# An AdaLN state-space block and six attention and feed-forward layers: output product in three rounded passes, Gelu from PSUM, new orders of the engines' queues, two state rows on GpSimd

## The reference

```python
def _L0_cond_ref(x, t_emb, ...):                # x (128, 32, 128), t_emb (128, 256)
    xr, gate = jnp.split(x @ W_in.T, 2, axis=-1)
    xr = xr + t_emb[:, None, :]
    xc = silu(causal_conv4(xr) + b_conv)
    xn = layernorm(xc) * ln_g + ln_b
    Bm, Cm, dt = jnp.split(xn @ W_xproj.T, 3, axis=-1)
    dt = jnp.tanh(dt @ W_dt.T + b_dt) * 0.01
    Ad, Bd = 1.0 + dt * (-jnp.tanh(A_log)), Bm * jnp.minimum(norm(xn), 1.0)
    h = jnp.clip(h * ad[:, :, None] + bd[:, :, None] * xt[:, None, :], -10.0, 10.0)   # 32 steps, 16 states x 256
    yt = jnp.einsum('bd,bdh->bh', ct, h)
    return (ys + D * xn) * silu(gate) @ W_out.T

def _L0_ffn_ref(x, ...):                         # 6 layers, 16 heads of 64, windows of 32
    for i in range(DEPTH):
        x = attn_layer(shift_tokens(x), Wqkv[i], q_scale[i], k_scale[i], Wo[i]) + x
        x = ffn_layer(shift_tokens(x), ln_g[i], ln_b[i], W1[i], b1[i], W2[i], b2[i]) + x
    return x
# attn_layer: l2-normed, scaled and rotated q and k; masked softmax of 8 q.k over the window; times v; @ Wo
# ffn_layer: layernorm, @ W1 (128 -> 2 x 341), a * gelu(gate), @ W2
x = x + _L0_ffn_ref(_L0_cond_ref(x, cond_2048, ...), ...)
```

## Time and profile before

| | us |
|---|---|
| median of 3 runs | 3040.13 (3039.28 to 3040.23) |
| profiled execution | 3038.72 |
| its span | 3036.9 |

### The profile page before, as it was taken

The page is one execution under the profiler, slowest core; times in us unless marked ns, Lnnn a source line. Parts: engine busy times, 40 slices in busy tenths (PEclk is TensorE's granted clock), DMA queues, the critical chain, the costliest instruction groups (busy, mean ns, idle before and its releaser), DMA issues. The chain is left out here.

```text
span 3036.9 us, 90328 instructions
## 1 busy us (share of the span) xinstructions
PE 2893.9 (95%) x35040; PEld 2002.2 (66%) x35040; DVE 2400.4 (79%) x3168; ACT 2425.5 (80%) x3783; POOL 2079.6 (68%) x1518
## 2 busy tenths in 40 slices
PE   8799978999999999999999999999999999999996
PEld 7688856666666666666666666666666666666662
DVE  7899967888788878778887787887788787888871
ACT  5788857888788888878788887878888887888872
POOL 6655557777777777677777677777777776776760
PEclk9899989999999999999999999999999999999997
DMA  1000011010011001010100110010110101100002
GB/s 51 22 1 1 1 28 29 23 26 23 23 32 34 23 20 26 24 38 23 26 23 22 33 31 25 21 26 24 28 33 23 26 23 26 28 21 21 18 20 64
DMA packets 72899, 76.58 MB, mean 25 GB/s; under 512 B 22937, under 2 KB 46551, under 8 KB 72663
## 3 DMA queue, kind: packets, MB, share of 16 engines
q1 hardware_dynamic: 71782, 74.01, 9.5%
q10 hardware_dynamic: 1008, 1.19, 0.2%
HBM read 22.71 MB, written 2.10 MB: 8 GB/s over the span
## 5 line engine op out<-in xcount | busy, mean ns | idle before, releaser
L1312 POOL TENSOR_TENSOR qk_r<-qk_r,qk_t 128x1024 f32<-128x1024 f32 x384 | 917.3, 2389 | 552.3 <-DVE qk_r L1168 388.0
L775 PE MATMUL pa<-w_hi,xs_hi 128*128 128x512 f32 x1152 | 577.1, 501 | 43.1 <-DVE qk_r L1168 26.1
L1161 DVE TENSOR_REDUCE ss<-sq 128x16 f32<-128x1024 f32 x384 | 463.5, 1207 | 18.7 <-ACT sq L958 18.4
L1177 DVE TENSOR_TENSOR qk_t<-pa,rot 128x1024 f32<-128x1024 f32 x384 | 465.4, 1212 | 0.0
L1168 DVE TENSOR_TENSOR qk_r<-pa,rot 128x1024 f32<-128x1024 f32 x384 | 465.3, 1212 | 0.0
L803 PEld LDWEIGHTS px<-ident_sb,qk_r 128*128 128x128 f32 x3072 | 350.9, 141 | 164.7 <-issue 100.4
L775 PE MATMUL pa<-w_hi,xs_lo 128*128 128x512 f32 x1152 | 455.8, 396 | 0.0
L775 PE MATMUL pa<-w_lo,xs_hi 128*128 128x512 f32 x1152 | 454.3, 394 | 0.0
L803 PE MATMUL px<-ident_sb,qk_r 128*128 128x128 f32 x3072 | 401.4, 274 | 30.7 <-POOL qk_r L1321 14.9
L1011 ACT COPY kT<-px 64x1024 f32<-64x1024 f32 x384 | 385.1, 1003 | 35.7 <-PE px L803 31.0
L1321 POOL TENSOR_TENSOR qk_r<-qk_r,inv 128x1024 f32<-128x1024 f32 x192 | 365.6, 1904 | 44.4 <-ACT inv L995 44.3
(11 more groups left out here) (145 smaller groups left out, 5431.0 us busy)
## 6 DMA issues: line engine op xcount, KB each, us to landing
pT<-prT SPq DMA_DIRECT2D x768, 64.0 KB, 2.0
w_part<-in_Wqkv SPq DMA_DIRECT2D x40, 192.0 KB, 2.6
wo<-in_Wo SPq DMA_DIRECT2D x6, 512.0 KB, 4.1
c_h<-in_x SPq DMA_DIRECT2D x4, 512.0 KB, 9.0
o_x<-in_x SPq DMA_DIRECT2D x8, 256.0 KB, 5.1
out<-o_out SPq DMA_DIRECT2D x8, 256.0 KB, 4.3
w<-in_W SPq DMA_DIRECT2D x6, 341.0 KB
spare<-in_Wqkv SPq DMA_DIRECT2D x1, 1536.0 KB, 6.3
```

Of the source, the lines that this page charges most:

```text
L775: last = pe.matmul(pa[(u + c) % 2][:, half * 512:half * 512 + 512], x[:, j * P:(j + 1) * P], w[:, at], start=(k == 0), stop=(k == 2))
L1161: dve.reduce_sum(ss[:, c, :], heads(sq[:]), AX.X).then_inc(s[sum_sem], 1)
L1177: dve.tensor_tensor(halves(qk_t[:, c, :]), halves(pa[(3 * j + c) % 2][:])[:, :, ::-1, :], table.unsqueeze(1).to_broadcast([P, HEADS, 2, DH ...
L1312: pool.tensor_tensor(qk_r[:, j % 2, c, :], qk_r[:, j % 2, c, :], qk_t[:, c, :], ALU.add)\
```

## The change

- The output product runs in three rounded passes. `copy_oT` writes the rounded outputs `oT_hi` (one buffer in place of two), and VectorE computes the rest (`rest_of_outputs`, from `px`) as `oT_lo`; `px` is free for the next query transposes when that is done. `Wo` is rounded once a layer by ScalarE (`round_wo`, in the first tile of the layer's second group) and its rest computed by GpSimd (`rest_of_wo`). The product's first half of the heads runs at the end of the fourth tile, its second half in the first tile of the next group.
- Gelu is applied straight from PSUM, block by block (`gate_gelu`); `tables` loads the Gelu table ahead of the first block and the other one behind the last. Scale and shift of the normalisation go from ScalarE to VectorE (`scale_shift`). The square of the centred values reads PSUM.
- The rotation of queries and keys on GpSimd moves into the tile's own iteration; all four compute queues have new orders in `body`. The keys' layout `kT` changes; their copy stays on ScalarE as two instructions.
- `group_steps` writes out the first two groups of every layer. Several buffers are shared or single (`fx`, `w_part`, `spare`).
- SP loads `Wo` after the four placements of iteration i with g == 0, now with tiles two back, and waits for `wo_lo_ready`.
- In the scan GpSimd does two state rows (`PS = 2`), VectorE adds the bias of dt (`dt_in`) in place of TensorE's product, and the first step's orders change.

```diff
-PS = 1
+PS = 2
...
-                        pe.matmul(pproj[:, 0:NPROJ], ones[0:32, :], dt_bias[:], start=True, stop=False)
...
                 def scale_bc(t):
                     if t < S:
-                        dve.wait_ge(s["dtt_ready"], t + 1)
+                        dve.wait_ge(s["proj_done"], t + 1)
+                        wait_for(dve, s["dtt_ready"], t - 1)
+                        dve.tensor_tensor(dt_in[:, t % 2, :], pproj[:, 2 * DS:NPROJ], bdt[:], ALU.add)\
+                            .then_inc(s["dt_ready"], 1)
...
-            new_layer(0)
-            body(0, 0, 0)
-            body(1, 0, 1)
-            with eng.Fori(2, GROUPS) as g:
-                body(g, 0, g)
-            for l in range(1, DEPTH):
+            for l in range(DEPTH):
                 new_layer(l)
-                with eng.Fori(0, GROUPS) as g:
+                for g in range(2):
+                    body(g + l * GROUPS, l, g)
+                with eng.Fori(2, GROUPS) as g:
                     body(g + l * GROUPS, l, g)
...
                 def body(i):
                     for j in range(GT):
...
+                        place_probs(i, j, 2)
 
                 for i in range(NG + 1):
                     body(i)
                     l, g = divmod(i, GROUPS)
                     if 0 < l < DEPTH and g == 0:
-                        sp.wait_ge(s["wo_done"], i)
+                        sp.wait_ge(s["wo_lo_ready"], l)
                         load_wo(l)
...
                         for hp in range(lo, hi):
-                            heads_out = oT[:, bass.ds(g % 2, 1), hp, :, :].rearrange("p o t n -> p (o t n)")
-                            last = pe.matmul(pg[:], wo[:, hp, :], heads_out, start=(hp == 0), stop=(hp == HP - 1))
+                            for k, (w, o) in enumerate(((wo_hi, oT_hi), (wo_hi, oT_lo), (wo_lo, oT_hi))):
+                                last = pe.matmul(pg[:], w[:, hp, :], o[:, hp, :, :].rearrange("p t n -> p (t n)"),
+                                                 start=(hp == 0 and k == 0), stop=(hp == HP - 1 and k == 2))
...
+                        act.activation(gt[0:m, k, :], pg[0:m, :], ACT.Gelu, bias=b1[0:m, 1, k:k + 1])\
...
+                def round_wo(l):
+                    act.wait_ge(s["wo_loaded"], 16 * (l + 1))
+                    wait_for(act, s["wo_done"], l * GROUPS)
+                    act.copy(wo_hi[:], wo[:]).then_inc(s["wo_hi_ready"], 1)
...
+                def scale_shift(i, back):
...
+                        dve.tensor_scalar(fx[:], fx[:], ln_par[:, 0:1], ln_par[:, 1:2], ALU.mult, ALU.add)\
+                            .then_inc(s["fn_ready"], 1)
+
+                def rest_of_outputs(i, j, back):
...
+                        dve.tensor_tensor(oT_lo[:, :, k, :].rearrange("p h (r q) -> p r h q", r=2),
+                                          px[:].rearrange("p (r h q) -> p r h q", r=2, h=HP),
+                                          oT_hi[:, :, k, :].rearrange("p h (r q) -> p r h q", r=2).bitcast(F32), ALU.subtract)\
+                            .then_inc(s["oT_lo_ready"], 1)
```

More of the change, by code:

```diff
@@ L824, in prefill_mask, with scores @@
                         pe.matmul(ps[:], ident_b[:], mask_b[:], start=True, stop=False, skip_group_check=True)
-                def scores(i, j):
-                    n, j, live = tile(i, j, 2)
+                def scores(i, j, back):
+                    n, j, live = tile(i, j, back)
                     if live:
@@ L904, in a_block, with down @@
                         at, m = HBLK[k]
-                        pe.matmul(pg[0:m, :], w1[:, at:at + m], fn[:], start=True, stop=True).then_inc(s["a_done"], 1)
-                def down(i):
-                    g, live = group(i, 2)
+                        pe.matmul(pg[0:m, :], w1[:, at:at + m], fx[:], start=True, stop=True).then_inc(s["a_done"], 1)
+                def down(i, back):
+                    g, live = group(i, back)
                     if live:
@@ L949, in _ @@
+                        weigh_values(i, j, 3, 1)
+                        if j == 1:
+                            a_block(i, 2, 0)
+                        if j == 2:
+                            down(i, 2)
+                        if j == 0:
+                            variance(i, 2)
                 group_steps(pe, body, lambda l: None)
@@ L1010, in copy_kT, with exponentials @@
                             rows = slice(half * DH, (half + 1) * DH)
[L1011 to L1015 removed]
+                            act.copy(kT[rows, half].rearrange("p h b j -> p (h b j)"), px[rows, :]).then_inc(s["tk_out"], 1)
+                def exponentials(i, j, back):
+                    n, j, live = tile(i, j, back)
                     if live:
@@ L1290, in _, with shift_lo @@
             def _(pool):
-                def shift_lo(i, back, half):
+                def shift_lo(i, back, half, first=False):
                     g, live = group(i, back)
+                    live = live and (first or not isinstance(g, int) or g > 0)
                     if live:
@@ L1305, in shift_lo, with rotate @@
                         pool.wait_ge(s["xs_ready"], 2 * chunk + 2)
-                def rotate(i, j, c, cos, sin, rotated):
-                    n, j, live = tile(i, j, 1)
+                def rotate(i, j, back, c, cos, sin, rotated):
+                    n, j, live = tile(i, j, back)
                     if live:
```

521 lines of the change are left out of this document (260 added, 261 removed).

## The result

The changed kernel takes 3188.7 us (median of four runs, 3188.1 to 3191.9) where the kernel before took 3040.2 (3039.3 to 3040.6) in the same comparison: a ratio of 1.049, with an interval of 1.048 to 1.051. I had forecast 3005 us, 35 us faster; it is 149 us slower, 184 us off, and outside my range of 2930 to 3070 us. The profiled execution took 3188.1 us with a span of 3186.2.

A forecast was written before the change was run, and what follows sets the result against it. TensorE was taken to bound the groups, with a short sum of waits. From 3038.7 us, -67 (groups), -17 (rotary tables), +63 and +1 (Wo), -8 (scan), -7 (ends), plus 1.4 to the median, gave 3005 us; range 2930 to 3070.

The forecast's parts named there:

- The orders: Engine queues in the 48 groups: waits sum as before, group 52.57 to 51.17 us, -67 us in all.
- the walk: Hand-timed period of four tiles in the new orders, queues strictly in order; trusted to 1 us per group, 48 in all.
- The output product: Eight full-precision products become 24 rounded passes: 1.4 us less TensorE per group; VectorE's subtraction adds 4.85 us.
- The feed-forward block: Joint Gelu of 1484 ns goes, table loads stay; VectorE's scale and shift 0.5 us, 0.8 more beside busy GpSimd.
- The layer starts: ScalarE waits for Wo before rounding, holding up TensorE: 12.7 us a layer, +63 us for five, +1 for layer 0.
- The gain of 17 us for the rotary tables: Layer starts: tables no longer precede a late GpSimd rotation, so most of 3.76 us goes, -17 us over five layers.
- The scan and the ends: Scan steps from 9.34 to 9.1 us, -8 us; the stack's first product and last two groups, together -7 us.
- (a): Groups: VectorE becomes the bound, its in-order waits decide; group 52.9 us, +16 in place of -67, 3089 us; chance 0.17.
- (b): Layer starts: Wo lands before ScalarE asks, or its rounding delays no one; without the 63 us, 2942 us; chance 0.14.
- (c): Groups: new orders also remove 1.5 of 2.2 us of waits; 49.7 us a group, 2933 us; chance 0.16.
- (d): Second tile: squares between two Gelus need another table, two more loads per group, up to +123, 3128 us; chance 0.03.
- my three signs of a wrong prediction: ScalarE not waiting for Wo; VectorE idle above 4 us a group; TensorE waiting for the subtraction at each tile's transposes.

The follow-up runs named there:

- e1_order: The changed kernel with the output product's second half directly behind the first, in the fourth tile: 3104.9 us.
- e12_hi3: e9_place with shift_hi of the second half moved from the next group's first tile to the fourth tile: 3018.0 us.
- e9_place: The changed kernel with Wo loaded a layer earlier and the output product's halves both in the fourth tile, the first moved forward behind the query transposes: 3053.2 us.
- e7_nosub: The changed kernel with the product's second half moved back and Wo loaded a layer earlier, without VectorE's subtraction of the outputs' rest: 3048.0 us.
- e13_ffnlate: e12_hi3 with shift_ffn put behind the query copy instead of ahead of it, in a group's first tile: 3013.5 us.
- e8_f32out: The changed kernel with the product's second half moved back, Wo loaded a layer earlier, and the output product in full precision: 3104.3 us.
- e10_gelu: e4_cond plus the Gelu part: each Gelu reads PSUM, with its table loaded ahead of the first: 3051.4 us.
- e2_load: The changed kernel with SP loading the next layer's Wo in the third group of the layer before: 3145.9 us.
- e4_cond: The kernel before with only the changed kernel's state-space (conditioning) block, two state rows on GpSimd: 3029.4 us.

## Why the prediction was wrong

**The orders: the step that failed.** I wrote that TensorE's waits "sum to what is waited now" and that "the groups lose the product's 1.4 us and nothing else". The usual group took 55.26 instead of 51.17: 4.1 us, 48 times, 196 us, more than the whole miss of 184, and four times the 1 us to which I trusted the walk. (At the layer starts the changed kernel lost 34 us on the kernel before, where I had +46; the other terms nearly held.) Two waits weren't in the walk:

- The outputs went from two buffers to one, and the wait of the copy from the product before last to the last one. In the same diff the second half of that product moved an iteration later. I priced each part and never put them together: a writer of tile 0 in the fourth iteration, a reader behind the next query projection. The copy stood 4.15 us, where the walk had none. Moving the half back gave 2.0 us a group (e1_order).
- ScalarE's queue in the first tile. The diff moves shift_hi's second half and shift_ffn there, ahead of the query copy. My list of orders has both, but none of the walk's waits is at the key transposes for that copy; they stood 84.9 us in all, 1.8 us a group. 0.7 us of the group came back when the first left again (e12_hi3), with 0.15 from the product's split (e9_place).

These make 2.8 of the 4.1 us. For the remaining 1.3 us, from 52.4 to 51.2, up to 0.2 may be VectorE's subtraction (e7_nosub); for the rest no run gives a cause. The windows show where it stands: TensorE's idle time is 0.80 us in the usual group before (52.57 less 51.77) and 1.62 in e13_ffnlate, in several waits of at most 0.39 us, for VectorE's rotary products and its subtraction, GpSimd's keys and the key copy. That is 0.8 of the 1.3 us, waits that I had as unchanged. I had put TensorE's own work at 50.3 before, so at 48.9 after; the trace shows TensorE busy for 50.8 in e13_ffnlate with 1.6 us of idle time, and busy time there holds modelled ends. How much of it is waiting stays open.

**The output product.** Right: passes start 0.23 us apart (1568.67, 1568.90 and on), and the difference of e8_f32out and e7_nosub is 1.35 us a group against 1.4. The subtraction takes 1195 ns against 1212 expected.

**The feed-forward block.** The scale and shift take 0.55 us in the median (I took 0.5), with a longest of 2.65 us, and 0.64 us in the mean, so the wait for GpSimd was rare; the 0.8 us was too much. For the Gelu part the walk had 0.75 us of waiting at the second gate product. By itself, in the orders of before, the part costs 0.47 us a group net, with a wait of 1.18 us there (e10_gelu). In the changed kernel that wait is smaller than I had walked, 9.7 us in all, 0.2 us a group.

**The layer starts.** The mechanism was right, by its own steps: SP's placements, Wo landing 4.4 us after its issue (4.1 expected), ScalarE idle for 8.56 us ahead of the rounding (about 9 expected). TensorE stood 8.32 us (6.7 expected) and its granted clock was 0.50 of full speed, the level of 1.2 GHz, in the 6 us behind (the columns are those of the windows above; the third from the right is the clock):

```profile
1350.00:1356.00 6.00, 3.50 (x9) 2.42 (x10) 3.06 (x3) 5.90 (x11) 1.90 (x1) 0.50 0.00 0
```

The term was 12.7 us a layer and was too large: the group is 10.5 us longer than a usual one, but 1.9 of these stay when the load is moved, so the wait itself measured 8.6, 43 us of the 63. The gain of 17 us for the rotary tables isn't separated by any run; with the load moved, two groups at a layer start still take 1.9 and about 0.2 us more than usual ones (57.15 and 55.49 in e2_load), where before they took 3.76 more.

**The scan and the ends.** Steps take 8.94 us (9.1 expected), diagonals ending at 266.42 and the clip starting at 266.49:

```profile
257.55 2.29 DVE L530 TENSOR_SCALAR c_h<-c_h 128x4096 f32<-128x4096 f32 x1
...
266.49 2.29 DVE L530 TENSOR_SCALAR c_h<-c_h 128x4096 f32<-128x4096 f32 x1
...
261.10 1.27 POOL L415 TENSOR_TENSOR c_h<-c_h,spare 128x512 f32<-128x512 f32 x1
...
262.81 3.61 POOL L433 TENSOR_TENSOR c_cdiag<-c_ident,c_bc 128x2048 f32<-128x2048 f32 x1
```

That holds from the fourth step on; the first three distances are 0.6 us shorter together. From the first clip to the last it is 11.6 us less, at the end of my bounds, and the part alone gave 12 us (e4_cond). My count had 0.6 us for the decay between GpSimd's second row operation and the diagonals; the rows have 0.44 (262.37 to 262.81). The ends came near their 7 us: TensorE stands 5.61 us in place of 8.33 ahead of its first product of the stack (2.7 less, 2.4 expected), and from the last but one variance product to the end of the span it is 3.4 us less (36.34 + 44.79 against 38.32 + 46.21).

**The rivals.** (a), VectorE as the bound, is refuted: with its 4.8 us gone the group shortened by 0.2 (e7_nosub). (b) and (c) did not happen. (d), which with 3128 us came nearest in time, is refuted: 96 table loads, two a group, none extra between the Gelus. Its mechanism in another form was real, a load that comes onto a path (e10_gelu). Of my three signs of a wrong prediction two fired: VectorE idle for 8.0 us a group, and TensorE waiting at px's transposes for the subtraction, 76.5 us in all, though at two of a group's eight sets only, and it was the copy ahead of the subtraction that was late. Of the chance of 0.24 for slower, 0.20 lay in (a) and (d), mechanisms that didn't occur, and none in a wait for the output product.

## What to carry to other kernels

When a diff halves a buffer, list at once who writes it next and who reads it last in the new order, and put both on one time axis; the lost buffer without the moved reader brings no such wait (e1_order), and the two together cost 2 us a group; the moved reader with both buffers was not run. On an in-order engine count the work of each stretch between two of its obligations, not of the period: ScalarE was idle 24% of a group and still late in its first tile. And taking 1.35 us of work off an engine made the group 0.47 us longer (e10_gelu), because a table load moved ahead of something that others wait for.

## What the runs showed of the hardware

A table load takes 1283 ns in the kernels before and after, and in e10_gelu the operations before and behind follow within 0.02 us (1477.94 + 0.32, 1478.27; 1478.27 + 1.28, 1479.57). The Trainium skill (ScalarE: Activation LUTs, What ACT_TABLE_LOAD costs) prices a change at about 2.66 us, about 1.28 for the load and the rest for a drain. The trace agrees on the load and shows no time for the drain. In the changed kernel squares and copies between two Gelus brought no further load (96 in 48 groups). The first large clip beside GpSimd's diagonals took 4.75 us with the diagonals starting at 99.91 and ending at 103.52, and the clip starting at 100.92: 2.15 us remain behind the diagonals' end, near the 2.29 of an undisturbed one, as in the earlier trace rows. The third clip did the same: 3.50 us from 122.23, with diagonals from 119.97 to 123.58.
